# Stores of edge sums grouped by slot number, and node rows gathered by an index, in a two-layer graph network with routed feed-forward stages

## What is computed

```python
x = x + L0_gnn(layernorm(x))   # attention over the edges of a node, 8 heads of 32, with edge features
x = x + L0_ffn(layernorm(x))   # 8 experts, the best two per row, gelu
x = x + L1_gnn(layernorm(x))   # attention over the edges, without edge features
x = x + L1_ffn(layernorm(x))   # 8 experts, the best one per row with a capacity, relu
```

```python
ex    = exp(alpha - segment_max(alpha, dst)[dst])
denom = segment_sum(ex, dst)
out   = segment_sum(h[src] * ex / denom[dst], dst) + bias
```

## Time and profile before

| | us |
|---|---|
| median of three timed runs | 7718.56 (7714.73 to 7724.49) |
| the profiled execution, span from first to last instruction | 7807.0 |
| the profiled execution, own time beside the span | not given |
| plan stage | 0 to 126 |
| node, edge, routing, expert stage of layer 0 | to 235, 3181, 3535, 4384 |
| node, edge, routing, expert stage of layer 1 | to 4487, 7087, 7348, 7807 |

### The profile page before, as it was taken

One profiled execution on the slowest core, in us unless ns is written; L12 is line 12 of the kernel. 1 busy time (PEld: TensorE's weight loads), 2 busy tenths in 40 slices (PEclk: granted clock), 3 DMA queues, 4 the chain that ended last, 5 costly groups with the idle time before them and its releaser, 6 DMA issues. The chain is left out here.

```text
span 7807.0 us, 99204 instructions
## 1 busy us (share of the span) xinstructions
PE 5257.7 (67%) x19729; PEld 3739.4 (48%) x19729; DVE 3278.9 (42%) x5938; ACT 1371.0 (18%) x2977; POOL 3613.4 (46%) x3708
## 2 busy tenths in 40 slices
PE   2387887788788878228999625556565556663498
PEld 1144444444444444227999514444444444442498
DVE  6255555555555555721111313333333333336244
ACT  2122222222222222002222200000000000000122
POOL 2635555555555554042222056666666666650222
PEclk9689999999999999658999857777777777786699
DMA  6434444444444443515666544444444444434255
GB/s 220 136 101 122 122 119 123 124 124 125 122 123 121 122 124 102 186 60 165 183 183 183 153 102 114 113 115 115 114 112 113 113 114 116 113 102 154 101 198 188
DMA packets 718013, 1022.24 MB, mean 131 GB/s; under 512 B 301733, under 2 KB 531561, under 8 KB 692608
## 3 DMA queue, kind: packets, MB, share of 16 engines
q0 software_dynamic: 183456, 485.95, 23.8%
q1 hardware_dynamic: 527676, 519.31, 21.7%
q10 hardware_dynamic: 6564, 14.14, 0.5%
HBM read 868.26 MB, written 153.27 MB: 131 GB/s over the span
## 5 line engine op out<-in xcount | busy, mean ns | idle before, releaser
L773 POOL DMA_INDIRECT e_rows<-sc_table,e_eidx x3224 | 3115.9, 966 | 2253.8 <-issue 952.6
L880 PE MATMUL e_ps_o<-e_rows,e_oh 128*128 128x264 f32 x6448 | 1918.5, 449 | 856.9 <-ACT e_res L969 700.8
L880 PEld LDWEIGHTS e_ps_o<-e_rows,e_oh 128*128 128x128 f32 x6448 | 1379.2, 222 | 1384.3 <-issue 1147.6
L1064 DVE SCALAR_TENSOR_TENSOR e_u<-e_encr,e_adst,e_ps_hd 128x512 f32<-128x512 f32 x806 | 597.1, 745 | 1160.2 <-remote 366.1
L1132 DVE TENSOR_TENSOR e_rows<-e_rows,e_ps_w 128x1024 f32<-128x1024 f32 x806 | 970.7, 1207 | 106.3 <-issue 83.5
L822 PE MATMUL e_ps_X<-e_u,e_hwide 128*104 128x512 f32 x1612 | 871.1, 635 | 16.8 <-DVE e_u L1064 14.8
L1055 DVE TENSOR_SCALAR e_ohT<-e_at,e_nid 96x512 bf16<-96x512 int16 x806 | 292.5, 363 | 1384.6 <-DMA e_aw<-sc_a2p 553.7
L969 ACT COPY e_res<-e_ps_o 32x264 f32<-32x264 f32 x806 | 296.0, 367 | 3291.4 <-PE e_ps_o L884 1242.4
L810 PE MATMUL e_ps_enc<-e_at,e_w_enc 96*128 96x512 bf16 x806 | 317.9, 394 | 570.6 <-ACT e_encr L942 383.4
L1676 PE MATMUL x_ps_h<-x_xT,x_w 128*128 128x256 f32 x2624 | 648.2, 405 | 15.4 <-DMA x_b<-in_L_ffn_b_dram 15.4
L1676 PEld LDWEIGHTS x_ps_h<-x_xT,x_w 128*128 128x128 f32 x2624 | 638.5, 337 | 20.6 <-issue 16.4
(11 more groups left out here) (290 smaller groups left out, 3538.7 us busy)
## 6 DMA issues: line engine op xcount, KB each, us to landing
x_w<-in_L_ffn_W_dram SPq DMA_DIRECT2D x112, 1024.0 KB
e_at<-sc_grp SPq DMA_DIRECT2D x403, 192.0 KB
x_w<-in_L_ffn_w_dram SPq DMA_DIRECT2D x60, 1024.0 KB
e_rows<-sc_table,e_eidx POOLq DMA_INDIRECT x3224
e_at<-sc_grp SPq DMA_DIRECT2D x403, 96.0 KB
sc_agg<-e_res SPq DMA_DIRECT2D x816, 33.0 KB
sc_xb<-r_zero SPq DMA_DIRECT2D x24, 1032.0 KB
x_xin<-sc_xb SPq DMA_DIRECT2D x86, 258.0 KB
```

The source lines that it names most:

```text
L773: pool.indirect_dma_start(rows[:, k, s, j, :], None, dr["table"][:, :], bass.IndirectOffsetOnAxis(eidx[:, k, s, j:j + 1], 0)).then_inc(s_r ...
L880: nc.tensor.matmul(ps_o[:, 0:ROW], oh[:, k, at_j:at_j + P], rows[:, k, s, j, :], start=(j == 0), stop=False)
L1064: nc.vector.scalar_tensor_tensor(u[:, p, h, :], encr[:, h, :], adst[:, h:h + 1], ps_hd[:, h, :], ALU.add, ALU.mult).then_inc(s_u, 1)
```

## The change

It numbers the rows of `agg` by slot: slot t has rows 32t to 32t+31, and no two slots overlap. So stores need no order among each other; three slots (`GROUPS`: 3, 3, 3, 3, 1 of a batch of 13) go out in one transfer, in steps 6, 9 and 12 of their own batch and 3 and 4 of the next, each after a wait for the eviction of its last slot only. ScalarE waits before evictions 0, 3, 6, 9 and 12 for the group that used the places. `blk` loses its third column, `agg` grows to 20512 rows of which 12896 to the end are zeroed, and SP's 31 stores after the loop become twelve.

A node's sum is now found by an index: `nrow[p, t]` is the row of node 128t + p, the last slot whose window starts at or before it, or a row of zeros. VectorE works it out once, in the last two batches of the first edge stage (which have no loads): two operations over 640 slots (`window_starts`), 49 comparisons that add up a code per node (`slots_of`, two per slot of the batch), and a chain of 11 small ones (`node_rows`); SP loads the starts before and stores the index after. In both routing stages POOL gathers the rows of `agg` by it, 49 transfers of 128 rows, in place of SP's seven loads.

The core of the diff:

```diff
@@ plan
-            for j in range(7):
-                act.dma_start(dr["agg"][j * 7 * P:(j + 1) * 7 * P, :].rearrange("(p j) d -> p (j d)", p=P), zero[:, :]).then_inc(s_st, 16)
-            act.dma_start(dr["agg"][NP:NP + WIN, :], zero[0:WIN, 0:ROW]).then_inc(s_st, 16)
+            for r0 in range(NG * WIN, ZROW + WIN, 7 * P):
+                n = min(P, (ZROW + WIN - r0) // 7)
+                act.dma_start(dr["agg"][r0:r0 + 7 * n, :].rearrange("(p j) d -> p (j d)", p=n), zero[0:n, :]).then_inc(s_st, 16)
@@ edge, SP
-            def store(t, s, n):
-                hold(sp, s_out, t * 16 - (32 * SB - OUT0), s_ps)
-                hold(sp, s_ev, t - (BEHIND - 1 - EV0), s_ps)
-                sp.dma_start(dr["agg"][bass.ds(n, WIN), :], res[0:WIN, kept((s - BEHIND) % SB), :]).then_inc(s_out, 16)
+            def store(b, g):
+                first_slot, end = GROUPS[g]
+                n, place = end - first_slot, kept(first_slot)
+                hold(sp, s_ev, b * SB + (EV0 + end), s_ps)
+                sp.dma_start(dr["agg"][bass.ds(b * (SB * WIN) + first_slot * WIN, n * WIN), :].rearrange("(s w) d -> w s d", w=WIN),
+                             res[0:WIN, place:place + n, :]).then_inc(s_out[g], 16)
...
-                    g, n, back = entry(t)
+                    g, n = entry(t)
                     load(ring(s), g, n)
-                    store(t, s, back)
+                    if s in (3, 4) and not isinstance(b, int):
+                        store(b - 1, s)
+                    if s in (6, 9, 12):
+                        store(b, s // 3 - 2)
...
-            for j in range(BEHIND):
-                t = steps * (2 * SB) + (3 * SB + j)
-                _, _, back = entry(t)
-                store(t, j % SB, back)
+            for j in range(3):
+                for g in range(len(GROUPS)):
+                    if j or g >= 3:
+                        store(steps * 2 + j, g)
+                if first and j == 0:
+                    hold(sp, s_xa, steps * (4 * SB) + 6 * SB, s_ps)
+                    sp.dma_start(starts, dr["nsf"][1:1 + TL].partition_broadcast(P)).then_inc(s_nst, 16)
+                    sp.dma_start(jumps, dr["nsf"][0:TL].partition_broadcast(P)).then_inc(s_nst, 16)
+            if first:
+                sp.wait_ge(s_row, 1)
+                sp.dma_start(dr["nrow"][:, :], nrow[:, :]).then_inc(s_nst, 16)
+                sp.wait_ge(s_nst, 48)
@@ edge, ScalarE
-                if not isinstance(t, int) or t + BEHIND - 2 * SB + 1 >= since(s):
-                    hold(act, s_out, t * 16 + 16 * (BEHIND - 2 * SB + 2 - since(s)), s_pa)
+                if s in (6, 9):
+                    hold(act, s_out[s // 3 - 2], b * 16 + 16, s_pa)
+                elif s in (0, 3, 12) and not (isinstance(b, int) and b == 0):
+                    hold(act, s_out[{0: 2, 3: 3, 12: 4}[s]], b * 16, s_pa)
@@ edge, VectorE
+            def slots_of(tile):
+                v.wait_ge(s_code, 2 + tile)
+                nc.vector.scalar_tensor_tensor(junk, starts, ncol[:, tile:tile + 1], jumps, ALU.is_le, ALU.mult,
+                                               accum_out=code[:, 0, tile:tile + 1]).then_inc(s_code, 1)
...
+                    if first and not pre:
+                        tile = (0 if turn else 2 * SB) + 2 * s
+                        if tile == 0:
+                            window_starts()
+                        for n in range(tile, min(tile + 2, NT)):
+                            slots_of(n)
+                        if NT - 2 <= tile < NT:
+                            node_rows()
@@ routing
+                sp.dma_start(nrow[:, :], dr["nrow"][:, :]).then_inc(s_nrow, 16)
...
-                    sp.dma_start(ag[:, c % 2, :, :], dr["agg"][c * R * P:(c + 1) * R * P, :].rearrange("(t p) d -> p t d", p=P)).then_inc(s_ag[c % 2], 16)
...
+                pool.wait_ge(s_nrow, 16)
+                for c in range(R):
+                    if c >= 2:
+                        pool.wait_ge(s_agu, c - 1)
+                    for r in range(R):
+                        pool.indirect_dma_start(ag[:, c % 2, r, :], None, dr["agg"][:, :],
+                                                bass.IndirectOffsetOnAxis(nrow[:, c * R + r:c * R + r + 1], 0)).then_inc(s_ag[c % 2], 16)
```

More of the change, by code:

```diff
@@ L46 @@
 EPS = 1e-5
[L47 removed]
+assert ZROW == TL * WIN and MAXSLOT <= (2 * MAXSTEP + 3) * SB and (2 * MAXSTEP + 4) * SB <= TL and PARTS * 8 == K3
 def semaphores(nc, ctx, prefix):
@@ L608, in edge_phase @@
             nodes, lags = miota, pm
+            ncol, code = sb("ncol", [P, NT], F32), sb("code", [P, 4, NT], F32)
+            nrow = sb("nrow", [P, NT], I32)
+            starts, jumps, junk = (u[:, :, :, :].rearrange("p a b e -> p (a b e)")[:, n * TL:(n + 1) * TL] for n in range(3))
             ps_enc = ps("ps_enc", [P, 512])
@@ L625, in edge_phase @@
             sem(n) for n in ("X", "y", "lk", "f", "b", "turn", "q", "f8", "mr", "mc", "al", "d", "col", "phi", "phb", "cf", "m"))
-        s_z, s_exp, s_wt, s_wc, s_sc, s_cs, s_o, s_ev, s_out = (sem(n) for n in ("z", "exp", "wt", "wc", "sc", "cs", "o", "ev", "out"))
+        s_z, s_exp, s_wt, s_wc, s_sc, s_cs, s_o, s_ev, s_nst, s_code, s_row = (
+            sem(n) for n in ("z", "exp", "wt", "wc", "sc", "cs", "o", "ev", "nst", "code", "row"))
+        s_out = [sem(f"out{g}") for g in range(len(GROUPS))]
         s_pv, s_pp, s_pa, s_ps, s_pg = (sem(n) for n in ("pv", "pp", "pa", "ps", "pg"))
@@ L642, in kept @@
             return s % KEEP if s < 2 * KEEP else KEEP
-        def since(s):
-            return SB - KEEP if s < KEEP else KEEP if s < 2 * KEEP else SB
         def behind(s):
@@ L740, in _ @@
                     phase(i * 2 + (1 + q), 1 - q)
-            for j in range(BEHIND):
-                t = steps * (2 * SB) + (3 * SB + j)
-                _, _, back = entry(t)
-                store(t, j % SB, back)
-            hold(sp, s_out, steps * (32 * SB) + (16 * SB + 16 * BEHIND + OUT0), s_ps)
+            for j in range(3):
[10 more added lines that the diff above has]
+                sp.wait_ge(s_nst, 48)
+            for g in range(len(GROUPS)):
+                hold(sp, s_out[g], steps * 32 + 48, s_ps)
             hold(sp, s_ei[1], steps * 16 + 32, s_ps)
@@ L794, in _ @@
         def _(pe):
-            pe.wait_ge(s_const, 9 if first else 6)
+            pe.wait_ge(s_const, 10 if first else 6)
             pe.wait_ge(s_ready, 1)
@@ L1134, in _, with window_starts, node_rows, after @@
             ahead = 1 if first else 0
+            def window_starts():
+                v.wait_ge(s_nst, 32)
+                nc.vector.tensor_tensor(jumps, starts, jumps, ALU.subtract).then_inc(s_code, 1)
+                v.wait_ge(s_code, 1)
+                nc.vector.tensor_scalar(jumps, jumps, float(CODE), None, ALU.add).then_inc(s_code, 1)
+                v.wait_ge(s_code, 2)
+            def slots_of(tile):
+                v.wait_ge(s_code, 2 + tile)
+                nc.vector.scalar_tensor_tensor(junk, starts, ncol[:, tile:tile + 1], jumps, ALU.is_le, ALU.mult,
+                                               accum_out=code[:, 0, tile:tile + 1]).then_inc(s_code, 1)
+            def node_rows():
+                count = [2 + NT]
+                def after(ins):
+                    count[0] += 1
+                    ins.then_inc(s_code, 1)
+                    v.wait_ge(s_code, count[0])
+                v.wait_ge(s_code, 2 + NT)
+                raw, cnt, off, has = (code[:, n, :] for n in range(4))
+                after(nc.vector.tensor_scalar(cnt, raw, 1.0 / CODE, -0.4, ALU.mult, ALU.add))
+                after(nc.vector.tensor_scalar(cnt, cnt, 12582912.0, None, ALU.add))
+                after(nc.vector.tensor_scalar(cnt, cnt, -12582912.0, None, ALU.add))
+                after(nc.vector.scalar_tensor_tensor(off, cnt, float(CODE), raw, ALU.mult, ALU.subtract))
+                after(nc.vector.tensor_tensor(off, ncol[:, :], off, ALU.add))
+                after(nc.vector.tensor_scalar(has, cnt, 0.0, None, ALU.is_gt))
+                after(nc.vector.scalar_tensor_tensor(has, off, float(WIN), has, ALU.is_lt, ALU.mult))
+                after(nc.vector.scalar_tensor_tensor(off, cnt, float(WIN), off, ALU.mult, ALU.add))
+                after(nc.vector.scalar_tensor_tensor(off, off, -float(WIN + ZROW), has, ALU.add, ALU.mult))
+                after(nc.vector.tensor_scalar(off, off, float(ZROW), None, ALU.add))
+                nc.vector.tensor_copy(nrow[:, :], off).then_inc(s_row, 1)
             def phase(b, k, pre, turn, turns, next_turns):
```

43 lines of the change are left out of this document (20 added, 23 removed).

## The result

The changed kernel takes **7764.18 us** (median of four runs, 7759.66 to 7767.33) where the kernel before, beside it, takes 7720.24 (7714.73 to 7724.49): a ratio of 1.0059, interval 1.0047 to 1.0072. It is slower by 44 us where 253 us less were forecast. In short: GpSimd's gathers, and not SP, set the pace of the second edge stage, so that fewer stores gave little there, and the routing stages pay more for their gathers than was forecast.

The account below looks back on a forecast made before the run. The prediction took SP's issuing to bound the second edge stage and TensorE nearly the first. Its terms, -170 - 100 + 12 + 1 + 4 = -253 us, taken from 7718.56 us, gave 7466 us, range 7260 to 7660.

Parts of the forecast that it names:

- So the second edge stage goes at SP's pace: Second edge stage: SP, issuing all loads and stores, waits only 6.6 us in 1800 and the other engines wait for it.
- -170: Second edge stage: fewer SP instructions cut a slot from 6.20 to 5.75 us over 377 slots; ends 0 and -340 us.
- slot holds four gathers, 5.05 us, the other 1.15 us POOL is paused: Second edge stage: split of a 6.20 us slot; SP does 6.4 instructions in the pause and 11.3 beside gathers.
- First edge stage, -100: First edge stage: evictions' 137.3 us of waits for stores mostly go, saving 100 us; ends 0 and -137.
- Its end, +12 and +1: Last two batches of the first edge stage: VectorE's index work adds 12 us, the index store 1 us.
- Routing, +2 each: Both routing stages: 49 POOL gathers replace seven SP loads, adding 2 us each, +4 together; ends -4 and +30.
- Planning, 0: Plan stage: zeroing 8.0 MB instead of 6.5 is hidden under VectorE's work, adding 0 us (-3 to +5).
- A: Rival, chance 0.15: POOL becomes the bound, a second-stage slot takes 5.3 us, first stage loses 137 us; 7258 us.
- B: Rival, chance 0.17: longer gather trains slow SP, second edge stage stays as now, first gains partly; 7645 us.
- C: Rival, chance 0.08: coarser stores come late, delaying evictions 6 and 9 in the second edge stage; 7900 us, lesser cases from 7760.
- D: Rival, chance 0.05: stores are late by transfer, not issue, so fewer issues give nothing; 7735 us.
- The base: Whole kernel: the forecast sum was taken from the timed median 7718.56 us, 1.1% under the profiled span 7807.

Follow-up runs that it names:

- a_gap: Changed kernel, GpSimd clearing 512 columns and waiting for that behind each slot's four gathers in the second edge stage: that stage 2636 us, a batch 81.9 us.
- a_short: Changed kernel, GpSimd clearing eight columns and waiting for that behind each slot's four gathers in the second edge stage: ratio 0.9980 to the kernel before.
- b_short: Kernel before, GpSimd clearing eight columns and waiting for that behind each slot's four gathers in the second edge stage: 7657.8 us, ratio 0.9910.
- a_two: Changed kernel with three routing buffers and GpSimd's eight-column clearing and wait behind every second slot of the second edge stage: ratio 1.0006 to the kernel before.
- a_nostore: Changed kernel without stores of sums, or waits for them, in the second edge stage: that stage 2543 us against 2547 with the same stage unchanged.
- a_bufs: Changed kernel with three buffers instead of two for the routing stages' gathered rows: ratio 0.9984 to the kernel before, routing stages 359.4 and 269.5 us.
- a_half: Changed kernel gathering rows of 528 bytes instead of 1056 in the second edge stage from its third batch: stage 2533.8 us, a batch 78.5 us.
- a_nowait: Changed kernel, GpSimd clearing eight columns behind each slot's gathers in the second edge stage without waiting for it: 7767.7 us in one run, a batch 78.5 us.
- b_two: Kernel before, GpSimd clearing eight columns and waiting for that behind every second slot of the second edge stage: ratio 0.9999, a batch 79.0 us.

## Why the prediction was wrong, point by point

**"So the second edge stage goes at SP's pace": this step failed.** It rested on the earlier trace rows. SP was never ahead, and loads were late (by its wait instructions VectorE waited 810 us for them, in the changed kernel 111; waits over 0.5 us), but little was lost by it: VectorE then waited 928 us for TensorE where it had waited 489, and GpSimd was the slower one. The 630.9 us of the earlier trace rows were 28.6 by the wait instruction. -170 was forecast; the stage got 29 to 45 us shorter, and without any store 4 more. The timelines did show the point, SP slow in long trains and quick in GpSimd's pause, but I read it as SP's trouble. It is everybody's: in such a train TensorE, VectorE and ScalarE stand still too. And the "slot holds four gathers, 5.05 us, the other 1.15 us POOL is paused" took the pause for slack to be won, where it is a cost that comes with the trains: some 13 us a batch with 52 gathers and with 39, and gone only in a_gap and mostly in a_short and b_short. What stops the other engines in a train stays open.

**First edge stage, -100: failed for the same reason.** The step was that a wait for a store which goes is time which goes. The waits of the earlier trace rows went to none, and the middle of the stage kept its pace (1148 gathers for 1147). On quick chips four kernels with single stores took 2897 to 2928 us there, three with grouped ones 2936 to 2943 and a fourth, a_two's slowest execution, 2969; 9 us are the next point. On the slow chip the two kinds can't be told apart: 2935, 2937, 2948 and 2973 us with single stores, 2940, 2953 and 2972 with grouped ones. So it did not get shorter; whether the change costs some 10 to 20 us more there is not shown, and no run tried it.

**Its end, +12 and +1: right in kind.** The last batch but one took 52.6 us (forecast 54), against 42.1 to 43.6 in the profiles with no index work; the last took 37.5 and hid the rest. The old one was 43.5 and not 42, so it cost 9.

**Routing, +2 each: wrong, +16 and +20.** VectorE's waits at its chunks, and of GpSimd's gathers the first chunk's last, the third's first and its last two, in the changed kernel:

```profile
3193.27 0.19 DVE L1479 TENSOR_SCALAR r_ag<-r_ag 128x56 f32<-128x56 f32 x1 [13.09 <-DMA r_ag<-sc_agg,r_nrow]
3217.35 0.34 DVE L1479 TENSOR_SCALAR r_ag<-r_ag 128x56 f32<-128x56 f32 x1 [2.97 <-DMA r_ag<-sc_agg,r_nrow]
3241.62 0.29 DVE L1479 TENSOR_SCALAR r_ag<-r_ag 128x56 f32<-128x56 f32 x1 [3.02 <-DMA r_ag<-sc_agg,r_nrow]
3267.62 0.19 DVE L1479 TENSOR_SCALAR r_ag<-r_ag 128x56 f32<-128x56 f32 x1 [4.81 <-DMA r_ag<-sc_agg,r_nrow]
```

```profile
3187.11 0.95 POOL L1401 DMA_INDIRECT r_ag<-sc_agg,r_nrow  x1 [0.30 <-issue]
...
3201.66 0.95 POOL L1401 DMA_INDIRECT r_ag<-sc_agg,r_nrow  x1 [4.55 <-DVEq L1499]
...
3207.93 2.67 POOL L1401 DMA_INDIRECT r_ag<-sc_agg,r_nrow  x1 [0.30 <-issue]
3210.91 1.75 POOL L1401 DMA_INDIRECT r_ag<-sc_agg,r_nrow  x1 [0.30 <-issue]
```

The terms that failed are two. The landing was put at 2 us from plain stores; the third chunk's last gather is issued by 3212.66 and its rows are there at 3217.35, 4.7 us on (the first's: 5.2). And the gathers do space out: two of these seven take 2.67 and 1.75 us beside VectorE's two operations of 128 x 1792 (2.03 us each). So a chunk asked for at 3201.66 came after 15.7 us, not 10.8. In the first routing stage: 3 us of later start, 11 of these waits, 2 of slower steps. Of the 98 gathers of both stages 12 take over 1.3 us, and these 12, and no others, begin beside a 128 x 1792 operation. The Trainium skill, "SBUF — State Buffer", section "SBUF: two separate sides", says that a VectorE operation with two SBUF inputs holds the shared ports, for the whole instruction, against a GpSimd operation that reads SBUF. The 2.67 us beside 0.95 agree if a gather counts as such an operation, which no run here tests apart. The Trainium skill, "DMA: Bandwidth & Descriptors", section on the anatomy of one DMA, fits 2.0 us plus bytes/436e3, an estimated 2.3 us for such a transfer; the trace shows 4.7 from the end of the last issue, behind others.

**Planning, 0: +3**, inside its bounds.

**Rivals.** A named the right engine and priced it without its pauses, at 5.3 us a slot; it is 5.02 (the prediction's 5.05) plus 1.0. B's mechanism, longer trains eat what SP gains, is what the runs showed, wider than I had it: the standstills of all engines grew from 461 to 584 us on the quick chips, from 441 to 542 on the slow one. C did not occur: 9.7 us of waits for stores. Its number, "lesser cases from about 7760", was met without it. D had 7735, and the routing stages' +36 for +4 bring the rest. It gave the stores nothing, which came true within some 40 us, but not by its reason: it put their lateness on the transfer, and a_nostore, which drops issue and transfer together, gains 4 us. The Trainium skill, "DMA: Bandwidth & Descriptors", section "Issuing engines are not separate DMA queues", says that the time to start a transfer is usually small beside the transfer; here SP took 13.5 us from one slot's load to the next, and that did not matter because GpSimd was slower. So C's and D's numbers were luck. D had 0.05, and no case joined "nothing gained" to "routing costs its upper bound", though the sum held both ends.

**The base.** A profile 1.1% above its kernel's runs should have been asked about: by its stage lengths it was a slow chip's, while the runs it was set against were a quick one's.

## What to carry to other kernels

Before work is taken from a queue that waits for nobody, ask of the next engine what its own issue costs, gaps included: 52 gathers of 1.256 us were 83% of a stage in which GpSimd looked 63% busy. A wait that a view puts on the last event proves little after a standstill; the engine's separate wait instructions tell which semaphore was late. And a gather in place of a plain load is to be priced with its landing behind other gathers (5 us here) and given one buffer more (21 us less in the two routing stages of a_bufs).

## What the runs showed of the hardware

- While GpSimd issues gathers without a pause in the second edge stage, the other engines stop 6.5 to 11 us into a train (four in five of the changed kernel's), and SP's register instructions take 0.70 us for 0.03; all resume together, a median 2.0 us after the last gather's issue. The bytes of the rows do not matter (a_half). A wait of GpSimd for a clearing of eight columns behind every four gathers takes most of it away (a_short from 28% of the stage to 9%, b_short from 22% to 13%, ratio 0.991), the clearing alone does not (a_nowait), and behind every eight gathers the wait gives nothing (b_two). Whether instructions or semaphore updates are what is held up was not settled: TensorE's update came 10 us after its matmul's end, but that end is modelled.
- A gather that begins beside a VectorE operation of 128 x 1792 with two SBUF inputs takes 1.75 to 2.67 us to issue for 0.95 (12 of 98 in the changed kernel's routing stages).
- The edge stages, 5540 us of the kernel, differ by some 70 us between chips; the other stages agree within 1 us.
